# Mamba heads' x turned by VectorE and a DRAM round trip instead of TensorE transposes, with the first handover reordered

## What is computed

```python
proj = hidden_states @ in_proj_w.T            # gate, hBC, dt
hBC = silu(causal_conv(hBC))                  # x, Bm, Cm
dt = softplus(dt + dt_bias)
x_dt = x * dt[..., None]
M = (Cm @ Bm.T) * exp(segment_sum(A * dt))    # token by token, lower triangle
y = M @ x_dt + D * x
y = y * rsqrt(mean(y * y) + eps) * norm_w * silu(gate)
out = y @ out_proj_w.T
```

## Time and profile before

| | |
|---|---|
| median of 3 runs | 619.64 us (619.43 to 620.79) |
| profiled execution, its own time | 619.38 us |
| its span | 617.6 us |
| PE busy | 602.9 us, 98% of the span |
| DVE, ACT, POOL busy | 417.6, 350.0, 308.9 us |
| DMA | 120.68 MB, mean 195 GB/s |
| chain that ended last | PE 77%, DVE 7%, POOL 6%, ACT 4%, issue 4%, DMA 2% |

### The profile page before, as it was taken

One profiled execution on the slowest core, in us unless ns is written; L12 is line 12 of the kernel. 1 busy time (PEld: TensorE's weight loads), 2 busy tenths in 40 slices (PEclk: granted clock), 3 DMA queues, 4 the chain that ended last, 5 costly groups with the idle time before them and its releaser, 6 DMA issues.

```text
span 617.6 us, 11024 instructions
## 1 busy us (share of the span) xinstructions
PE 602.9 (98%) x3934; PEld 531.5 (86%) x3934; DVE 417.6 (68%) x875; ACT 350.0 (57%) x619; POOL 308.9 (50%) x213
## 2 busy tenths in 40 slices
PE   8999999999999999999999999998999999999997
PEld 7888888899998889899988989987989988898573
DVE  5433147678888888888886668698473573748783
ACT  4403125577776867686676635664846667467110
POOL 0000011369778877887786712257578486492000
PEclk9999999999999999999999999998999999999999
DMA  8301021878887788788778929753867757698500
GB/s 350 143 0 35 1 68 38 216 190 214 214 212 201 200 213 213 200 204 214 179 179 222 348 108 310 287 179 134 300 239 281 272 196 283 256 365 333 201 1 17
DMA packets 29694, 120.68 MB, mean 195 GB/s; under 512 B 7712, under 2 KB 8224, under 8 KB 22096
## 3 DMA queue, kind: packets, MB, share of 16 engines
q1 hardware_dynamic: 28912, 118.96, 61.9%
q10 hardware_dynamic: 576, 1.05, 0.5%
q0 software_dynamic: 160, 0.07, 0.1%
HBM read 86.30 MB, written 0.26 MB: 140 GB/s over the span
## 4 chain that ended last, share of the span: by engine, by line
PE 77%; DVE 7%; POOL 6%; ACT 4%; issue 4%; DMA 2%; DVEq 0%; ACTq 0%; SPq 0%; POOLq 0%
PE ps L1878 16%; PE ps L1582 13%; PE ps L1583 12%; PE ps L1584 12%; PE ps L1680 4%; PE ps L1913 3%; POOL pt_lo L578 3%; PE ps L1756 3%; PE ps L1924 2%; PE ps L2061 2%; PE ps L1623 2%; PE ps L1640 2%; DMA ring<-w_out_dram 2%; POOL v_lo L578 2%; PE ps L2024 2%
## 5 line engine op out<-in xcount | busy, mean ns | idle before, releaser
L578 POOL TENSOR_TENSOR pt_lo<-far_t,pt_hi 128x512 fp32r<-128x512 f32 (+1 forms) x94 | 111.8, 1216 | 54.9 <-ACT pt_hi L729 54.7
L1878 PEld LDWEIGHTS ps<-norm_t,ring 128*128 128x128 f32 x1152 | 131.6, 192 | 2.7 <-issue 1.3
L1878 PE MATMUL ps<-norm_t,ring 128*128 128x128 f32 x1152 | 133.2, 276 | 0.0
L811 ACT ACTIVATE prob_far<-prob_far,neg_max 128x1024 f32<-128x1024 f32 (+2 forms) x96 | 85.5, 892 | 54.8 <-DVE neg_max L1231 54.8
L1227 DVE TENSOR_SCALAR_CACHE_REDUCE prob_far<-ps 128x256 f32<-128x256 f32 (+2 forms) x96 | 86.7, 906 | 32.2 <-PE ps L1584 31.7
L1408 DVE SCALAR_TENSOR_TENSOR acc<-ps,cw,acc 128x127 f32<-128x127 f32 (+2 forms) x240 | 63.3, 340 | 18.1 <-ACT acc L984 17.9
L1251 DVE STREAM_TRANSPOSE prob_far<-prob_far 128x2176 f32<-128x2176 f32 x30 | 73.1, 2436 | 0.8 <-ACT prob_far L811 0.2
L578 POOL TENSOR_TENSOR v_lo<-v_all,v_hi 128x256 fp32r<-128x256 f32 (+2 forms) x12 | 16.7, 1395 | 102.9 <-ACT v_hi L729 102.9
L1582 PE MATMUL ps<-pt_hi,v_hi 128*128 128x256 f32 x208 | 61.2, 294 | 2.6 <-POOL pt_lo L578 2.3
L1582 PE MATMUL ps<-k_hi,q_hi 128*128 128x512 f32 (+2 forms) x160 | 61.4, 384 | 1.4 <-ACT v_all L729 0.7
L1584 PE MATMUL ps<-pt_lo,v_hi 128*128 128x256 f32 x208 | 58.8, 283 | 0.0
(11 more groups left out here) (255 smaller groups left out, 1267.6 us busy)
## 6 DMA issues: line engine op xcount, KB each, us to landing
ring<-w_in_dram SPq DMA_DIRECT2D x36, 1024.0 KB, 4.8
far_t<-prob_far SPq DMA_DIRECT2D x240, 136.0 KB, 2.7
ring<-w_out_dram SPq DMA_DIRECT2D x16, 1024.0 KB, 4.9
ring<-wq_dram SPq DMA_DIRECT2D x16, 512.0 KB, 4.1
ring<-wo_dram SPq DMA_DIRECT2D x16, 512.0 KB, 3.7
w_sb<-w_dram SPq DMA_DIRECT2D x4, 896.0 KB, 8.9
ring<-ctx_t_dram SPq DMA_DIRECT2D x3, 1024.0 KB, 4.9
ring<-w_dram SPq DMA_DIRECT2D x3, 1024.0 KB, 9.0
```

The source lines that it names most:

```text
L578: sub = lambda dst, a, hi: pool.tensor_tensor(dst, a, hi, ALU.subtract)
L811: nc.scalar.activation(tile, tile, ACT.Exp, bias=neg_max[:, b, h:h + 1], accum_out=part_sum[:, b, h, i:i + 1]).then_inc(exp_ok, 1)
L1878: ins = mm(ps[:, bank, t * T:t * T + T], w[:, t, c, :], norm_t[:, c, :], start=(c == 0), stop=(c == NC - 1))
```

## The change

PE's transposes of x are kept for group 0 alone. For groups 1 to 7:

- DVE, after the second convolution chunk, turns xc in 32x32 blocks (`turn_x`) into `x_turn`, a view of both `acc` buffers.
- SP (`x_moves`) sends it to a DRAM scratch `x_by_blocks` in one transfer of 512 KB, waits until this has landed, and fetches it back in four transfers of 128 KB, one for each 32 partitions, into the new tile `x_tok`, tokens on the partitions. `x_moves(g)` stands between `out_load(g-1, 1)` and `in_load(g, 2)` on SP.
- `x_times_dt(g)` reads `x_tok` (SBUF) and a copy of dt in PSUM bank 7, in two instructions of 512 elements instead of one of 1024.
- ACT's `first_tap` of `acc[0]` waits until x is back (`x_there`), since it writes over `x_turn`.
- At the first handover DVE turns x(1) before the masks of group 1, and does `x_times_dt(1)` and mask (2, half 0) before `gate(0)`; PE's segments (2, half 0) wait for the exponentials of group 1 (`dec_ok`) and no longer for its masks; ACT and POOL split the two halves of the first output chunk around it in another order.
- The copy of c2 on ACT moves from ahead of `mamba_step(5)` into it, behind the two `conv_silu`; `w1_split(2)` on ACT moves behind the last `gate_out` and waits for the last `xdt`.

```diff
+            def x_moves(g):
+                sp.wait_ge(x_turned, g)
+                sp.wait_ge(xdt_ok, g)
+                sp.dma_start(x_dram, x_turn).then_inc(x_out, 16)
+                sp.wait_ge(x_out, 16 * g)
+                for j in range(4):
+                    sp.dma_start(x_tok[32 * j:32 * j + 32, :, :, :].rearrange("k i t c -> k i (t c)"),
+                                 x_dram.rearrange("(i k) j t c -> j k i (t c)", k=32)[j, :, :, :]).then_inc(x_there, 16)
...
             with sp.Fori(2, GROUPS - 1) as g:
                 in_load(g, 0)
                 in_load(g, 1)
                 out_load(g - 1, 0)
                 out_load(g - 1, 1)
+                x_moves(g)
                 in_load(g, 2)
                 in_load(g, 3)
...
             for g in (GROUPS - 2, GROUPS - 1):
+                if g == GROUPS - 1:
+                    x_moves(GROUPS - 1)
                 for i in range(2):
                     out_load(g, i)
...
+                act.wait_ge(x_there, X_MOVED * g)
+                first_tap(step_chunk(g, 0), k, 0, 8 * g + 8, 0)
...
+                if low_rank:
+                    act.wait_ge(stack_in, 96)
+                    copy(c2_st[:], c2_sb[:]).then_inc(c2h_ok, 1)
...
                 if last:
+                    act.wait_ge(xdt_ok, GROUPS)
+                    w1_split(2)
                     w1_split(3)
...
+            def turn_x(g, b):
+                dve.wait_ge(silu_ok, 2 * g + 6)
+                nc.vector.transpose(x_turn.rearrange("p j t k -> p t j k"),
+                                    xc[b][:].rearrange("p t (j k) -> p t j k", k=32)).then_inc(x_turned, 1)
...
             def x_times_dt(g):
-                dve.wait_ge(xt_ps, g + 1)
-                nc.vector.tensor_tensor(xdt[:], ps[:, 4:6, :].rearrange("p a (h c) -> p (a h) c", c=64),
-                                        dt[:, bass.ds(g * HPG, HPG)].unsqueeze(2).to_broadcast([P, HPG, 64]),
-                                        ALU.mult).then_inc(xdt_ok, 1)
+                dve.wait_ge(x_there, X_MOVED * g)
+                dve.wait_ge(dt_home, 1)
+                for odd in range(2):
+                    heads = ps[:, 7, bass.ds(g * HPG, HPG)].rearrange("p (t o) -> p o t", o=2)[:, odd, :]
+                    ins = nc.vector.tensor_tensor(
+                        xdt[:].rearrange("p (t o) (i c) -> p o i t c", o=2, c=32)[:, odd, :, :, :],
+                        x_tok[:, 2 * odd:2 * odd + 2, :, :],
+                        heads.unsqueeze(1).unsqueeze(3).to_broadcast([P, 2, TPG, 32]), ALU.mult)
+                ins.then_inc(xdt_ok, 1)
...
             skip_add(0, 0)
+            turn_x(1, 1)
             mask_decay(1, 1, 0)
             mask_decay(1, 1, 1)
+            x_times_dt(1)
+            mask_decay(2, 0, 0)
             gate(0, 0)
-            x_times_dt(1)
...
                 taps_of(k + 1, 1, 8 * g + 12, 1)
+                turn_x(g + 1, o)
                 gate(g, b)
...
             def mamba_step(g, before_g, b, first):
-                x_transposes(g, b)
                 segments(g + 1, 1 - b, 0)
```

More of the change, by code:

```diff
@@ L252, in build @@
                 bc = sbuf(st4, "bc", [P, 16, T])
+                x_tok = sbuf(st4, "x_tok", [P, 4, TPG, 32])
                 gm = sbuf(st4, "gm", [P, GROUPS, T])
@@ L261, in build @@
                     final = sbuf(st5, "final", [P, DM])
-                acc = [sbuf(st4, f"acc{b}", [P, 4, T]) for b in range(2)]
+                acc_all = sbuf(st4, "acc", [P, 2, 4, T])
+                acc = [acc_all[:, b, :, :] for b in range(2)]
+                x_turn = acc_all[:].rearrange("p b c t -> p (b c t)").rearrange("p (j t k) -> p j t k", j=4, k=32)
                 xc = [sbuf(st4, "xc0", [P, TPG, T])]
@@ L544, in _ @@
                 in_load(0, j)
+            def x_moves(g):
[6 more added lines that the diff above has]
+                                 x_dram.rearrange("(i k) j t c -> j k i (t c)", k=32)[j, :, :, :]).then_inc(x_there, 16)
             out_load(0, 0)
             out_load(0, 1)
-            for j in range(4):
-                in_load(1, j)
+            in_load(1, 0)
+            in_load(1, 1)
+            x_moves(1)
+            in_load(1, 2)
+            in_load(1, 3)
             with sp.Fori(2, GROUPS - 1) as g:
@@ L697, in out_low, with first_out_low @@
                         out_hi1b[:].bitcast(F32)).then_inc(outl_ok, 1)
+            def first_out_low():
+                lo, w = ring_lo[out_chunk(0, 1)[0]], ring[out_chunk(0, 1)[0]]
+                pool.wait_ge(ug_ok, 2)
+                pool.wait_ge(outh_ok, 2)
+                sub(lo[:, SLOT // 2:SLOT], w[:, SLOT // 2:SLOT], out_hi1b[:].bitcast(F32))
+                u_low(0)
+                pool.wait_ge(outh_ok, 3)
+                sub(lo[:, 0:SLOT // 2], w[:, 0:SLOT // 2], out_hi1a[:].bitcast(F32)).then_inc(outl_ok, 1)
             def u_low(g):
@@ L1068, in w1_split, with mamba_step @@
                 copy(w1_hi[:, c, :], w1_sb[:, c, :]).then_inc(w1h_ok, 1)
-            def mamba_step(g, b, last=False, handover=False):
+            first_out, first_before = out_chunk(0, 1)
+            def mamba_step(g, b, last=False, handover=False, low_rank=False):
                 k, o = 2 * g + 6, 1 - b
@@ L1073, in mamba_step @@
                 if handover:
+                    act.wait_ge(landed[first_out], (first_before + 1) * 16)
+                    copy(out_hi1b[:], ring[first_out][:, SLOT // 2:SLOT]).then_inc(outh_ok, 1)
+                act.wait_ge(x_there, X_MOVED * g)
+                first_tap(step_chunk(g, 0), k, 0, 8 * g + 8, 0)
+                if handover:
                     u_high(0)
                     act.wait_ge(ysq_ok, 1)
-                    out_high(0, 1)
-                first_tap(step_chunk(g, 0), k, 0, 8 * g + 8, 0)
+                    copy(out_hi1a[:], ring[first_out][:, 0:SLOT // 2]).then_inc(outh_ok, 1)
                 decay_exp(g + 1, o, 1)
@@ L1089, in mamba_step @@
                 gate_out(step_chunk(g, 2), 0, sg[o][:, 0:4, :])
-                if last:
-                    w1_split(2)
-                else:
+                if not last:
                     out_high(g, 1)
@@ L1102, in _ @@
                     mamba_step(turn * 2 + (i + 1), 1 - i)
[L1103 to L1105 removed]
+            mamba_step(5, 1, low_rank=True)
             mamba_step(6, 0, True)
@@ L1886, in segments @@
                         pe.wait_ge(dec_ok, 2 * g + half)
+                elif isinstance(g, int) and g == 2 and half == 0:
+                    pe.wait_ge(dec_ok, 4)
                 else:
@@ L1894, in segments, with first_x_transposes @@
                 mm(ps[:, 3, :], upper_r[:], los, start=False, stop=True).then_inc(seg_ps, 1)
[L1896 to L1902, removed]
+            def first_x_transposes():
+                pe.wait_ge(silu_ok, 2)
                 for t in range(TPG):
-                    ins = nc.tensor.transpose(ps[:, 4 + t // 4, (t % 4) * T:(t % 4 + 1) * T], xc[b][:, t, :], ident[:])
+                    ins = nc.tensor.transpose(ps[:, 4 + t // 4, (t % 4) * T:(t % 4 + 1) * T], xc[0][:, t, :], ident[:])
                 ins.then_inc(xt_ps, 1)
@@ L1909, in y_product @@
                 pe.wait_ge(xdt_ok, g + 1)
+                if isinstance(g, int) and g == 1:
+                    pe.wait_ge(y_ok, 1)
+                elif not (isinstance(g, int) and g == 0):
+                    pe.wait_ge(ug_ok, 2 * g)
                 pe.wait_ge(m_ok, 2 * g + 2)
```

24 lines of the change are left out of this document (17 added, 7 removed).

## The result

The changed kernel takes **645.49 us** in the median of four runs (644.55 to 646.27), beside 619.53 us for the kernel before: a ratio of 1.0414, with a 95% interval of 1.0394 to 1.0435. That is 26 us slower. The prediction had 625.2 us and a range up to 631.0: right in sign, and far off in size.

The account below looks back on a forecast made before the run. PE, busy 98% of the span (DVE 68%), was taken as the bound. Steps +3.3, handover +0.5 and end +2.0 gave +5.8 us on the profiled 619.38: 625.2 us, with an 8-in-10 range of 617 to 631 us.

Parts of the forecast that it names:

- Transposes, 6.1 us off PE: Mamba steps: removing seven groups of eight transposes, 0.87 us each group, takes 6.1 us off PE.
- fast rival: Store does not queue, x is back 1.3 us into the step, ACT's exponential sets the mask: 617.5 us, chance 0.22.
- Turn 1.2 us, products 1.3, mask 1.22: DVE's added or chained work in a step: turning xc 1.2 us, two half products 1.3, then the mask 1.22.
- The store, and with it x's return: In a step, store queued behind the second output load lands at 492.6; after 3.9 us of fetches x returns 3.3 us in.
- I take 4.9: Landing time chosen for the output load ahead of the store: the median 4.9 us, though this load took 5.6.
- PE waits 1.8 us: Each step g = 2 to 6: mask done 6.0 us in, PE wants it at 4.2; five waits make 9.0 us.
- The clock: Slower rival: half clock follows PE's waits, two to four drops in the five steps, 628.5 to 632 us; chance 0.22.
- 1.66 us each: Cost of one half-clock drop on PE, from y_product taking 3.63 us instead of 1.97.
- No wait shortens the next: Steps: all counted from where project(g, 1) ends, so a wait in one step does not shorten the next; five waits add up.
- Handover, +0.5 us: First handover: x(1) turned from 413.72, empty queue, PE restarts at 424.4 instead of 423.90, +0.5 us.
- The moved gate and the split halves are off this path: Handover: mask (2, half 0) stands behind the DRAM trip, no longer the gate, so these reorderings do not affect PE's restart.
- The end, +2.0 us: Group 7: ACT's w1 split waits for xdt, delaying DVE's split, skip_add and PE's out_proj(7, 0), +2.0 us.

Follow-up runs that it names:

- no_trip: Changed kernel without the DRAM store, the four fetches and all waits for them; products read a constant tile instead of x: 611.04 us, 0.9855.
- reorder_only: Kernel before plus all the change's edits except the trip; PE's transposes stay, handover reordered, c2's copy inside step 5: 614.59 us, 0.9914.
- warm12: Changed kernel with 12 idle matmuls on PE ahead of the second segments of each step, to keep its clock up: 635.78 us, 1.0269.
- trip_unread: Changed kernel with store and fetches still running, but DVE's products read a constant tile and never wait for x: 623.82 us, 1.0059.
- store_before_load: Changed kernel with SP issuing the store ahead of the second output load and the fetches behind that load: 646.36 us, 1.0448.
- mask_first_y_late: Changed kernel with DVE's mask ahead of the products and, on PE, y_product behind project(g, 1): 621.97 us, 1.0040.
- best1: mask_first_y_late plus POOL's first low part not waiting for ug, second input load behind the trip, DVE's w1_split(2) share behind the last gate: 634.0 us, 1.0227.

## Why the prediction was wrong

- *Transposes, 6.1 us off PE.* Not contradicted, and not measured alone. no_trip is 3.55 us under reorder_only: the transposes less the mask waits that come up in their place, 2.0 us against 0.8, and less whatever the turn costs. That leaves 1.3 of the 6.1 us unexplained. The prediction's fast rival had this effect ("ACT's exponential sets the mask").
- *Turn 1.2 us, products 1.3, mask 1.22.* Right: 1.25, 1.29 and 1.22 us.
- *The store, and with it x's return.* Landing late behind the load was right, 2.6 us at the handover (416.21 to 418.81), 6.0 in the median behind a load. "I take 4.9" for the output load was the wrong choice: with the trip in the traffic that load landed after 5.7 us in step 3, and the store 1.35 us after it, as the 1.3 said. The 5.6 of the earlier trace rows was the row at hand, and it stood there as the bound. (The 3.2 us that the prediction estimated for a lone store come from a fit that the Trainium skill, DMA: Bandwidth & Descriptors, Anatomy of one DMA, gives for DMAs issued from GpSimd; this one was issued from SP and took 2.6 us.) The fetches took 4.3 us to the product, not 3.9. So x came 4.7 us into step 3 and 4.8 to 6.3 into the others, and not 3.3 (step 2's store took 7.8 us, step 4's 6.7), and **"PE waits 1.8 us"** measured 2.6 to 4.3. Five waits, 15.9 us, against 9.0: the term was short by 6.9 us. That is the first step that failed.
- *The clock.* The text gave it 0.22 as a rival with two to four drops, since 1.8 us lay just below the 1.93 us that had been followed by half clock. With waits of 2.6 us and more every step had its drop, and so had the end. **"1.66 us each"** holds for the four stretches of 3.4 us (1.7 too many in each) and not for the three of 6.8 us, in which PE worked 5.1 to 6.1 us (2.5 to 3.0 too many). warm12 gave back 9.7 us net, some 13 by its rows. This is the second, and the larger, failure: the sum had nothing for it, where the estimate is 13.5 us. With the 6.9 of the waits it makes up nearly all of the 20.3 us between 625.2 and 645.49. The two are one chain, since the wait as forecast lay on the right side of the only row on the clock.
- *No wait shortens the next.* "SP's next two loads slip by 4 us, but their slots are not read for most of a step" was right for PE's input loads. But the output loads' landing is waited for by ACT, whose exponential stands behind it. That path was not in the text; trip_unread shows it, as part of the 12.8 us that the moves cost unread.
- *Handover, +0.5 us.* PE restarted at 425.50 where the text had 424.4, but the turn began at 414.94 and not at 413.72, since this execution was 1.1 us late before the Mamba layer began. From the turn to the restart it was 10.6 us, where the text had 10.7: the term was right. The clock's drop stayed, as said, but twice as long (6.8 us instead of 3.4). What the text missed is that the reorder by itself is a gain: with the trip taken away it brings 2.94 us and the 1.66 of the drop. "The moved gate and the split halves are off this path" was wrong for the kernel without a trip, and so the fast rival was probably mispriced at 617.5: no_trip, which has no trip at all, ran in 611.04.
- *The end, +2.0 us.* Half right. ACT's split waited for xdt and skip_add stood behind DVE's half, as said (in trip_unread PE waits 4.20 us for last_ug). But in the changed kernel PE "loses hardly anything" was wrong: it waited 2.2 us for xdt, had half clock, and did not have to wait for last_ug after that. From the start of out_proj(6) to the next layernorm's transposes it took 23.3 us (591.28 to 614.60), against 20.3 from x's transposes on (567.83 to 588.12): +3.0.
- *The chances and range.* The range reached to three drops at 1.66 us each and to no longer wait than 1.8. The two unknowns were tied, and the case with both was in no rival.

The store that isn't held up, the fast rival, is refuted in its first step: 6.0 us to landing. In store_before_load even a store of 3.0 us did not make the change win, because the fetches then stood behind the output load, and ACT waited for that load.

What stays open: the 1.3 us of the transposes; why the trip took longest in steps 2 and 4; and what decides the clock (below).

## What to carry to other kernels

Where an engine at 98% is relieved by a DMA round trip, count the trip from the producer's last instruction to the consumer's first with the landing times of a loaded queue, take the worst of the rows at hand and not the median, and put whatever else does not need it ahead of the instruction that waits for it (here the mask: 19 us). A wait on TensorE has to be priced with the stretch at half clock that can follow, for each occurrence (1.7 to 3.0 us here); a single row on record does not say from which length on. And when an edit comes in a bundle, time the rest without it: here 5.5 us of gain sat unseen beside 31 us of loss.

## What the runs showed of the hardware

A wait's length alone does not decide on PE's clock. After waits of 2.63 and 2.75 us in the changed kernel there was half clock, but trip_unread stayed at full clock after 3.32 us, and mask_first_y_late after 3.01 us:

```profile
524.00:527.00 3.00, 2.84 (x36) 2.25 (x36) 2.01 (x9) 1.92 (x4) 3.00 (x2) 1.00 0.99 418
```

```profile
430.00:433.00 3.00, 2.73 (x12) 2.23 (x13) 3.00 (x10) 2.11 (x2) 3.00 (x3) 1.00 0.65 276
```

And in best1 half clock (0.51 from 535.2 to 538.6) followed a wait of 0.58 us, with one of 1.09 us that had ended 1.5 us earlier:

```profile
535.12 5.43 PE L1936 MATMUL ps<-norm_t,ring 128*128 128x128 f32 x32 [0.58 <-DMA ring<-w_in_dram]
```

The traffic is not it either. The DMA share was as high (0.99) in the first row above, at full clock, as in the slow stretches, and store_before_load had half clock at a share of 0.27:

```profile
513.00:516.00 3.00, 2.86 (x15) 2.12 (x17) 2.76 (x12) 1.14 (x2) 1.79 (x3) 0.50 0.27 112
```

What does decide it, no run here shows. And a DMA issued from an empty queue of another engine landed no sooner (6.2 us against 6.0) than one behind a 1 MB load in the same queue.
